# Edge-pair visits of graph layer 1: one 128-column matmul with 260 columns, against four of 32 weight columns with 65 columns each

## The reference

```python
h = (x @ W).reshape(n, heads, ch)
es = (h * a_src).sum(-1)
ed = (h * a_dst).sum(-1)
e = jax.nn.leaky_relu(es[src] + ed[dst], SLOPE)
m = jax.ops.segment_max(e, dst, num_segments=n)
w = jnp.exp(e - m[dst])
den = jax.ops.segment_sum(w, dst, num_segments=n)
alpha = w / den[dst]
msg = h[src] * alpha[:, :, None]
out = jax.ops.segment_sum(msg, dst, num_segments=n)
```

## Time and profile before

| what | value |
|---|---|
| time, median of 3 runs | 1429.63 us (1427.03 to 1445.0) |
| span of the profiled execution | 1433.1 us |
| PE busy | 1235.7 us (86%) |
| PE weight loads busy | 949.4 us (66%) |
| DVE busy | 857.0 us (60%) |
| ACT busy | 689.2 us (48%) |
| POOL busy | 739.1 us (52%) |
| layer 1's steps | about 106 to 626 us of the span |
| layer 2's steps | about 645 to 990 us |
| experts | about 1026 to 1430 us |

### The profile page before, as it was taken

One profiled execution on the slowest core, in us unless ns is written; L12 is line 12 of the kernel. 1 busy time (PEld: TensorE's weight loads), 2 busy tenths in 40 slices (PEclk: granted clock), 3 DMA queues, 4 the chain that ended last, 5 costly groups with the idle time before them and its releaser, 6 DMA issues.

```text
span 1433.1 us, 21729 instructions
## 1 busy us (share of the span) xinstructions
PE 1235.7 (86%) x6317; PEld 949.4 (66%) x6318; DVE 857.0 (60%) x2543; ACT 689.2 (48%) x1833; POOL 739.1 (52%) x652
## 2 busy tenths in 40 slices
PE   1667699889989999947888989994699999999997
PEld 1346455455645555426766768773699999999996
DVE  8369898788789988733566857687422222222221
ACT  1258676656676776733333334341434344334432
POOL 4600478675767774016666666630144445454544
PEclk9689899999999999967999989996799999999999
DMA  8003743643563372054545554534033332323221
GB/s 244 4 5 96 202 112 103 185 120 82 146 163 111 104 208 73 27 195 122 158 129 169 171 173 137 165 102 115 12 94 94 95 98 37 95 37 97 35 37 27
DMA packets 138053, 156.89 MB, mean 109 GB/s; under 512 B 59695, under 2 KB 117440, under 8 KB 137976
## 3 DMA queue, kind: packets, MB, share of 16 engines
q0 software_dynamic: 34528, 73.04, 21.0%
q1 hardware_dynamic: 101344, 81.57, 18.5%
q10 hardware_dynamic: 2104, 1.38, 0.4%
HBM read 121.19 MB, written 35.52 MB: 109 GB/s over the span
## 4 chain that ended last, share of the span: by engine, by line
PE 63%; DVE 20%; issue 9%; DMA 3%; ACT 2%; another core or an unknown queue 1%; POOL 1%; DVEq 0%; POOLq 0%; SPq 0%; ACTq 0%
PE bank L1317 12%; PE bank L1437 12%; PE bank L1445 12%; PE bank L1389 10%; PE bank L1268 10%; DVE ring_a L1924 4%; DVE ohk L1652 3%; DVE ohs L1648 2%; PE bank L1300 2%; DMA out_x<-ring_a,si 1%; DVE st L1533 1%; PE bank L1176 1%; ACT ring_a L1038 1%; PE bank L1411 1%
## 5 line engine op out<-in xcount | busy, mean ns | idle before, releaser
L796 POOL DMA_INDIRECT arena<-rows,idx_e x365 | 409.9, 1123 | 250.7 <-issue 110.4
L1317 PE MATMUL bank<-ring_a,slots 128*65 128x384 f32 (+1 forms) x1000 | 336.0, 459 | 34.0 <-DVE ring_a L1924 29.3
L1038 ACT ACTIVATE ring_a<-vbb,slots 128x384 f32<-128x384 f32 (+1 forms) x500 | 243.8, 562 | 16.0 <-DMA vbb<-v_rows 10.7
L1317 PEld LDWEIGHTS bank<-ring_a,slots 128*65 128x65 f32 x1000 | 131.8, 143 | 150.2 <-issue 100.1
L1389 PE MATMUL bank<-h2t,ring_a 128*128 128x257 f32 x700 | 186.1, 408 | 21.3 <-issue 17.0
L1146 ACT ACTIVATE ring_a<-bank,cols 128x128 f32<-128x128 f32 x432 | 128.6, 371 | 157.5 <-PE bank L1437 157.2
L1924 DVE SCALAR_TENSOR_TENSOR ring_a<-ring_a,arena 128x1536 f32<-128x1536 f32 (+1 forms) x125 | 191.9, 1536 | 17.2 <-ACT ring_a L1038 8.7
L1268 PE MATMUL bank<-arena,ring_a 128*128 128x257 f32 (+1 forms) x730 | 174.0, 385 | 3.0 <-issue 2.0
L1389 PEld LDWEIGHTS bank<-h2t,ring_a 128*128 128x128 f32 x700 | 137.3, 204 | 47.6 <-issue 24.1
L1268 PEld LDWEIGHTS bank<-arena,ring_a 128*128 128x128 f32 x730 | 140.1, 192 | 33.5 <-issue 8.1
L843 POOL DMA_INDIRECT gs<-gates,gk x54 | 51.4, 951 | 150.3 <-DVE gk L2076 144.5
(11 more groups left out here) (301 smaller groups left out, 1629.4 us busy)
## 6 DMA issues: line engine op xcount, KB each, us to landing
counts_all<-arena SPq DMA_DIRECT2D x14, 800.0 KB
arena<-counts_all SPq DMA_DIRECT2D x14, 800.0 KB
arena<-in_L_ffn_W SPq DMA_DIRECT2D x8, 1024.0 KB, 7.6
vbb<-v_pairs SPq DMA_DIRECT2D x23, 320.0 KB
arena<-rows,idx_e POOLq DMA_INDIRECT x365
XB<-general_sums SPq DMA_DIRECT2D x38, 130.0 KB
vbb<-in_L_ffn_W SPq DMA_DIRECT2D x4, 1024.0 KB
spare<-in_L_ffn_W SPq DMA_DIRECT2D x4, 1024.0 KB
```

The lines of the kernel that those rows point to most:

```text
L796: pool.indirect_dma_start(to[:, k, 0:width], None, table, bass.IndirectOffsetOnAxis(idx_e[:, m * PAIR + k:m * PAIR + k + 1], 0)).then_inc( ...
L1038: ins = act.activation(S1[q % SLOTS1][:, h * k * P:(h + 1) * k * P].rearrange("p (t n) -> p t n", n=P), vb1[:, 0:k, h, :], ACT.Copy, scale ...
L1317: pe.matmul(bank[h][0:CH + 1, 0:w_], slots[:, s, h * (CH + 1):(h + 1) * (CH + 1)], S1[q % SLOTS1][:, h * w_:(h + 1) * w_], start=(s == 0), ...
```

## The change

In layer 1 each block of an edge pair is four matmuls in place of one. The matmul of head h takes the 32 weight columns of that head and its 65 moving columns, and writes partitions 32h to 32h+31, columns 65h to 65h+64 of the same bank: the four parts that are read, and nothing else. The last of the four increments `s_pv`, so that the semaphore counts as before. Layer 2 keeps its code under the name `pair2`. Waits, buffers, transfers and the work of all other engines are the same.

```diff
-            def pair(n, width, weights_of, sums, start, stop):
+            def pair2(n, weights_of, sums, start, stop):
                 for k in range(PAIR):
-                    pe.matmul(sums[:, 0:width], weights_of(k), slot_of(n)[0][:, k, 0:width],
+                    pe.matmul(sums[:, 0:W2T], weights_of(k), slot_of(n)[0][:, k, 0:W2T],
                               start=(start and k == 0), stop=(stop and k == PAIR - 1)).then_inc(s_pv, 1)
 
             def edge_pair1(p):
                 wait_bank(("pair", p))
                 pe.wait_ge(s_pw, p + 1)
-                pair(p, W1T, lambda m: W1C[p % 2][m], bank_of(("pair", p)), True, True)
+                sums = bank_of(("pair", p))
+                for m in range(PAIR):
+                    for h in range(HEADS):
+                        r, c = slice(h * PW, (h + 1) * PW), slice(h * (CH + 1), (h + 1) * (CH + 1))
+                        ins = pe.matmul(sums[r, c], W1C[p % 2][m][:, r], slot_of(p)[0][:, m, c], start=(m == 0), stop=(m == PAIR - 1))
+                    ins.then_inc(s_pv, 1)
```

More of the change, by code:

```diff
@@ L1360, in edge_pair2 @@
                 pe.wait_ge(s_pw, PAIRS + p + 1)
-                pair(PAIRS + p, W2T, lambda m: W2[k][:, m, :], bank[4 + t % 2], k == 0, p == last_pair2(t))
+                pair2(PAIRS + p, lambda m: W2[k][:, m, :], bank[4 + t % 2], k == 0, p == last_pair2(t))
             def hooks2(q):
```

## The result

The changed kernel took 1459.3 us (median of 4 runs, 1450.3 to 1467.0), the kernel before 1432.3 (4 runs): a ratio of 1.0154, 95% interval 1.0109 to 1.0199. The forecast was 1410, so the change went 1.5% the other way.

The account below looks back on a forecast made before the run. PE was taken to bound layer 1, DVE close behind. Of 30 us freed on PE, 15 plus 5 us pass to the end: 1429.6 to about 1410 us, forecast's own range 1403 to 1418, overall range 1394 to 1450.

Parts of the forecast that it names:

- That strips overlap: Layer 1 visits on PE: the four heads' matmuls run side by side, a block taking 0.26 us in place of 0.438.
- full overlap: Rival, layer 1 visits: loads of different strips also run side by side, block about 0.13 us, time near 1392; chance 0.12.
- The switch: Before and behind each layer 1 visit: changing the array's division costs 0.11 us each way, 0.22 a visit.
- The sum on PE: Layer 1 visits: 1.54 us each against 2.19, 0.65 less; over 46 visits 30 us of PE.
- The serial rival: Layer 1 visits: four matmuls run one behind the other, 0.31 to 0.51 us more a visit, 1442 to 1449; chance 0.29.
- From PE to the end: Layer 1: of 30 us freed on PE, 15 pass in the full stretches and 5 elsewhere, together 20 us.
- ACT and POOL wait for visits and are released a little earlier: Layer 1, engines behind PE's visits: their waits end a little earlier; no size of its own given.
- The clock: Stretches with visits: granted clock should stay 1.00 where it is; a drop to 1.2 GHz would make the forecast wrong.
- Layer 2 and the experts keep their times: Stages outside layer 1, which the change does not touch: no change in time.

Follow-up runs that it names:

- One strip: Changed kernel with all four heads' matmuls writing partitions 0 to 31, one behind the other; 1386.8 us (1 run), prompt session, kernel before 1378.6.
- prompt sessions: Sessions of runs in which the kernel before takes 1379 to 1380 us; the change has a ratio of 0.9911 there.
- two strips: Against the changed kernel, 64 weight columns with 130 columns each, 20 records a visit in place of 40; ratio to before 0.9894 prompt, 0.9957 late.
- the wide matmul: Against the kernel before, one matmul of 128 weight columns with only 65 columns a block, array never divided; 1356.6 us, ratio 0.9847, prompt session.
- late sessions: Sessions of runs in which the kernel before takes 1432 to 1448 us; the change has ratios of 1.0154 and 1.0156 there.

## Why the prediction was wrong

**That strips overlap: right, and by more.** The choice on which everything hung went the right way, but the forecast chose the wrong bound. It took one weight load at a time, 0.26 us a block; a block takes 0.113 us, the bound of the "full overlap" rival (0.13), which had a chance of 0.12. The loads of 32 columns are recorded with 105 to 112 ns each and still start 6 to 9 ns apart, so they too run side by side. The Trainium skill ("TensorE: Matmul & The Clock Gate", Part 3) has 2.38 times for three strips of 512 columns; here the four, with 65 columns, reach 4.1 times the pace of one. Its rule in the same part, that loads overlap running matmuls only where the row group differs, does not hold for these rows.

**The switch: right.** From the dense record's start to the visit's it is 0.416 us against 0.323, so 0.093 us in; out of it 0.152 against the strip's own 0.057, so 0.095. The forecast had 0.11 each way.

**The sum on PE: mis-sized.** 0.65 us a visit and 30 us forecast; 1.39 us and 64 us measured (61 in the rival).

**The serial rival: its price was right, its premise not.** One strip costs 0.32 us a visit more than before in the step from dense to what follows (2.831 against 2.514); the rival had 0.31 to 0.51. Its floor, that no record would fall under 57 ns, held within one strip (58 ns) and not across four (14 ns a record).

**From PE to the end: the step that failed.** It read: "DVE, at 186.7 of 210 us, leaves 23 us, so nearly all passes", and for full overlap 38 us of 61. In prompt sessions two strips free 38 us and layer 1 keeps 11; the wide matmul frees 52 and keeps 16; the change frees 64 and keeps 10. So a third passed at best, and less the more PE was freed, where the forecast passed on 20 of 30. The prompt traces, added up from start to start between the first and the last dense matmul, say where it went: PE is idle 19.7 us more before the dense matmuls (32.6 to 52.3), mostly for DVE, and 15.6 us more before the one-hot ones (8.5 to 24.1), and the records that are not visits take 18.3 us more, with 59 us at the 1.2 GHz level in place of 31. That leaves 64 - 19.7 - 15.6 - 18.3 = 10, as measured. The busy shares of DVE were no measure of what it could take: in the five full stretches it is busy 180.6 us after the change (51.88 + 22.48 + 28.51 + 54.54 + 23.17), less than the 186.7 before, since its work comes in an order in which it waits in turn for others. No mark of a bound was to be read from its share. That the change has 0.991 in a prompt session, near the forecast's 0.986, is luck: twice the PE time was freed, and a sixth of it passed in place of two thirds.

**"ACT and POOL wait for visits and are released a little earlier": false in the late sessions, and this turned the sign.** A visit ends 1.4 us sooner there but is reported 2.6 us behind its end, and so 1.2 us later than before. The idle time of PE before the one-hot matmuls, which need ACT's copies, grew by 34.2 us in place of 15.6, and PE stood still inside or ahead of visits for 4.2 us more. ACT's wait did not fall but rose, from 72.4 us in 36 waits (2.0 each) to 76.8 in 25 (3.1 each). No step of the prediction had a price for telling others that PE is done, and in layer 1 of before there was nothing to see of one (0.04 us). In its layer 2 there was.

**The clock.** It was named as what could go wrong, for the wrong reason (an array mostly idle). From 345 to 380 us it stayed at 1.00, visits and all, with PE busy 87%; it is lowest, 0.86, from 545 to 570 us, where PE is busy least, 69%. The one strip, with three quarters of the array idle in its visits, has 0.957 over its run beside 0.951 to 0.956 for before. The wide matmul, which never divides the array, has 0.943 to 0.946, about as low as four strips (0.937 to 0.954). So the drop goes with a PE that waits more, not with strips.

**"Layer 2 and the experts keep their times": right in the first comparison** (333.3 and 334.7 us in layer 2). In other late sessions single traces of layer 2 lie between 334 and 351 us, whatever the visits of layer 1 were, and between kinds of session it differs by 41 us.

**What stays open.** What makes a session late, and what behind PE takes in the reports. Two things speak for a path that is shared with the recording of the trace. In prompt sessions the trace holds all 1962 increments that PE makes (before and change), in late ones 1710 to 1821. And of all semaphore events it holds 20,400 in prompt sessions and 12,400 to 12,800 in late ones, of which the landings of transfers are 14,600 and 7,500 to 8,000, while instructions and transfer packets are complete in both. Against it stands that the times without a full profile are the same as those with one (1466 to 1472 us beside 1472.9 in the late session). But every run lists a clock, so I can't say that any was free of recording. The clock is no rival for layer 1 of the kernel before: it has 31 to 32 us at the 1.2 GHz level in either kind of session. Shown are the delay, its growth in layer 1 with the instructions of a dense run, that it needs no strips, that it is PE's signals alone, and that PE itself stands still some 130 instructions into such a run. Argued only is that PE is stopped by the reports.

## What to carry to other kernels

Narrow column strips of the array do run side by side, loads included, and a result of which only diagonal blocks are read can be had for a quarter of the matmul time. But count the instructions as well as the columns: a change that puts four times as many into a quarter of the time should be tried in a milder form beside it (two strips, or a burst split by other work), and in more than one session. Look in the trace at when the increments come, not only at when the matmuls end. And price the way from a faster engine to the end by what waits behind its signals, in order, on the next engine, not by the next engine's idle share.

## What the runs showed of the hardware that was not expected

- Four float32 matmuls of 32 weight columns and 65 moving columns, in four column strips, take 113 ns together with their eight loads, where one strip takes 58 ns for each of eight records. The Trainium skill ("TensorEngine Tiling (Array Packing)", Instruction Overhead) speaks of some 60 cycles for each matmul; here, across four strips, a record adds 14 ns, 34 cycles at 2.4 GHz.
- Changing from 128 columns to strips and back costs 0.093 and 0.095 us.
- In late sessions PE's increments fell behind the matmuls, by up to 2.8 us in the visit shown and by up to 13 us in layer 2 of the kernel before, while those of ACT and DVE were on time. In the visit they came out at about 90 ns an instruction, and then in a row 34 to 43 ns apart. PE ran ahead of them until some 130 instructions into one dense run, and then took three or four records in each 0.75 us.
- The same kernel differs by 4 to 5% between sessions, and a change can have opposite signs in them (0.991 and 1.015, intervals apart).
